# One decoder block on one core: every engine's calls in another sequence, and the table of logarithms read only when another was read since

## What is computed

```python
x = x + attention(layernorm(x))        # 16 heads of 32, one shared K and V, windows of 128 in steps of 64
x = x + wkv(w, u, layernorm(x), ctx)   # a recurrence over the tokens, per channel
x = x + ffn(layernorm(x))              # 512 -> 2048 -> 512
# attention, per window:
Q, K = Q * cos + rotate_half(Q) * sin, K * cos + rotate_half(K) * sin
K, V = quant_dequant_8bit(compress(K)), quant_dequant_8bit(compress(V))
p = sigmoid(Qw @ Kw.T * scale);  wout = p / (p.sum(-1) + 1e-8) @ Vw      # neighbouring windows are blended
# ffn: activations are rounded to 8 bits per row, weights to -1, 0, 1 by the mean of their magnitudes
h = silu(linear(x, w_gate)) * linear(x, w_up);  out = linear(rms_norm(h), w_down)
```

## Time and profile before

| what | value |
|---|---|
| runs | 1063.14, 1063.1 and 1060.24 us, median 1063.1 |
| profiled execution, its span | 1062.2 us |
| PE busy | 867.7 us (82%) |
| DVE busy | 854.9 us (80%) |
| ACT busy | 660.2 us (62%) |
| POOL busy | 454.9 us (43%) |

### The profile page before, as it was taken

The page is one execution under the profiler, slowest core; times in us unless marked ns, Lnnn a source line. Parts: engine busy times, 40 slices in busy tenths (PEclk is TensorE's granted clock), DMA queues, the critical chain, the costliest instruction groups (busy, mean ns, idle before and its releaser), DMA issues.

```text
span 1062.2 us, 22082 instructions
## 1 busy us (share of the span) xinstructions
PE 867.7 (82%) x8388; PEld 522.0 (49%) x8388; DVE 854.9 (80%) x1630; ACT 660.2 (62%) x1162; POOL 454.9 (43%) x494
## 2 busy tenths in 40 slices
PE   6984646769888889888888888888898988986665
PEld 3453434445555555555545555555555555553222
DVE  4766495998979897988979898979897879797944
ACT  0237654564949595858576767667676757584633
POOL 1111113155453645363636364646464535445522
PEclk9996667979999999999999999999999999998978
DMA  9977251210606151515142323232323223032032
GB/s 339 412 240 270 82 196 41 68 41 11 147 21 137 31 138 29 137 31 112 56 92 71 82 81 87 81 87 81 87 81 86 82 56 111 29 103 49 21 60 69
DMA packets 119386, 107.17 MB, mean 101 GB/s; under 512 B 91792, under 2 KB 94720, under 8 KB 118128
## 3 DMA queue, kind: packets, MB, share of 16 engines
q1 hardware_dynamic: 116320, 100.64, 32.6%
q0 software_dynamic: 624, 2.59, 0.8%
q10 hardware_dynamic: 2336, 2.52, 0.7%
HBM read 65.62 MB, written 10.75 MB: 72 GB/s over the span
## 4 chain that ended last, share of the span: by engine, by line
PE 43%; DVE 17%; ACT 15%; issue 11%; DMA 6%; POOL 2%; SPq 1%; DVEq 0%; ACTq 0%; POOLq 0%
PE bank L513 11%; PE bank L602 10%; PE bank L612 7%; PE bank L543 5%; PE bank L532 5%; ACT arena L742 3%; DMA wide<-wide 3%; ACT junk L799 2%; ACT junk L804 2%; DVE amax L1143 2%; DVE wide L1034 2%; DVE wide L1060 1%; DVE fs L1186 1%; PE bank L583 1%; ACT L742 1%
## 5 line engine op out<-in xcount | busy, mean ns | idle before, releaser
L602 PE MATMUL bank<-w_up_gate,qT 128*128 128x512 bf16 x1024 | 241.1, 387 | 28.3 <-DMA qT<-q_tok 22.0
L1378 POOL TENSOR_TENSOR work<-junk,lnw 128x512 f32<-128x512 f32 x128 | 180.7, 1431 | 183.5 <-DVE junk L1177 161.4
L602 PEld LDWEIGHTS bank<-w_up_gate,qT 128*128 128x128 bf16 x1024 | 98.7, 99 | 144.0 <-DMA qT<-q_tok 23.3
L513 PE MATMUL bank<-wide,wq_sb 128*128 128x256 f32 x512 | 131.1, 421 | 28.1 <-DVE rows L1078 28.1
L612 PE MATMUL bank<-w_down,work 128*128 128x512 bf16 x512 | 121.5, 383 | 22.5 <-ACT junk L799 13.3
L513 PEld LDWEIGHTS bank<-wide,wq_sb 128*128 128x128 f32 x512 | 107.8, 213 | 57.2 <-issue 39.7
L1177 DVE TENSOR_TENSOR junk<-bank,junk 128x512 f32<-128x512 f32 x128 | 86.2, 683 | 59.3 <-PE bank L602 55.5
L799 ACT ACTIVATE junk<-bank,deq 128x512 f32<-128x512 f32 x128 | 85.6, 686 | 72.2 <-PE bank L602 71.6
L742 ACT ACTIVATE arena<-bank 128x384 f32<-128x384 f32 x256 | 104.8, 496 | 33.7 <-PE bank L532 33.5
L532 PE MATMUL bank<-wide,k_win 32*128 32x128 f32 x1536 | 69.1, 315 | 61.3 <-ACT arena L742 38.2
L564 PE MATMUL bank<-wo_sb,wide 128*128 128x512 f32 x256 | 117.0, 611 | 2.5 <-DVE wide L1071 2.5
(11 more groups left out here) (154 smaller groups left out, 1478.0 us busy)
## 6 DMA issues: line engine op xcount, KB each, us to landing
sums<-in_xT SPq DMA_DIRECT2D x8, 1024.0 KB, 10.9
wide<-in_xT SPq DMA_DIRECT2D x16, 512.0 KB, 4.3
wide<-wide SPq DMA_DIRECT2D x64, 128.0 KB, 2.1
out<-rows SPq DMA_DIRECT2D x32, 256.0 KB, 2.3
ctx_T<-in_ctxT SPq DMA_DIRECT2D x15, 512.0 KB, 5.0
rows<-in_x SPq DMA_DIRECT2D x15, 512.0 KB, 3.2
kv_b<-k_raw SPq DMA_DIRECT2D x64, 96.0 KB, 2.4
work<-in_wgT SPq DMA_DIRECT2D x4, 1024.0 KB, 7.5
```

Source lines behind the costliest of these rows:

```text
L513: last = te.matmul(in_bank(k, 2)[:, n % 2, :], wq_sb[:, c, n * P:(n + 1) * P], xT[:, c, :], start=c == 0, stop=c == NC - 1)
L602: last = te.matmul(bank[4 + k % 4][:, :], qT[:, c, t * P:(t + 1) * P], w_up_gate[:, m, c, cols], start=c == 0, stop=c == NC - 1)
L1378: ge.tensor_tensor(hid_w[:, t, cols], hid[:, n % 2, :], lnw[:, cols], op=ALU.mult).then_inc(z_set.sem, 1)
```

## The change

Every engine gets its calls in another sequence; none is added or removed, but for table loads. `log_tables()` is now called by each function that needs the table (`logs`, `inverses`, `wkv_logs`, `wkv_inverses`, `exps`), and does nothing if that table was the last one read. The call stands ahead of the function's waits, as before.

```diff
+        held = [None]
+
         def probs(b, c):
+            held[0] = None
...
         def log_tables():
-            se.add_instruction(mybir.InstLoadActFuncSet(name=nc.get_next_instruction_name(),
-                                                        engine=mybir.EngineType.Activation, act_func_set_id=LN_EXP))
+            if held[0] != LN_EXP:
+                se.add_instruction(mybir.InstLoadActFuncSet(name=nc.get_next_instruction_name(),
+                                                            engine=mybir.EngineType.Activation, act_func_set_id=LN_EXP))
+            held[0] = LN_EXP
 
         def logs(b, c):
+            log_tables()
...
         def silu(f, t, n):
+            held[0] = None
```

On DVE, the tail of a round and the start of the next:

```diff
+            if i == 2:
+                round_weights(DOWN, 0)
             if do_f:
+                wkv_norm(f)
+            if do_g:
+                peak(g, 1)
+            if i == 2:
+                round_weights(DOWN, 1)
+            if do_f:
+                wkv_quantise(f)
...
+            if do_w:
+                residual(w)
...
+            if i == 2:
+                round_weights(DOWN, 2)
+            if do_w:
+                att_norm(w)
+            if do_f:
                 hidden(f, 0, 0)
+            if do_g:
+                hidden_round(g, 1)
...
+            if do_f:
+                hidden(f, 0, 1)
             if do_b:
                 rope(b, 0)
                 rope(b, 1)
...
+            if do_w:
+                scan(w, 0)
             if do_b:
                 rotate(b, 0)
-            if do_w:
-                scan(w, 0)
...
                 rotate(b, 1)
```

On POOL, the sum of the third weight:

```diff
             if do_f:
                 hidden_rstd(f, 0)
+            if i == 1:
+                weight_total(DOWN)
...
                 weigh_hidden(w, 0, 0)
-            if i == 0:
-                weight_total(DOWN)
-            if do_w:
                 weigh_hidden(w, 0, 1)
```

More of the change, by code:

```diff
@@ L621, in tensor_program @@
             do_b, do_w, do_f, do_g = [0 <= n < B for n in (b, w, f, g)]
+            if do_g:
+                gate_up(g, 1, 1)
+            if do_w:
+                nums(w, 2)
+            if do_g:
+                gate_up(g, 1, 2)
+            if do_w:
+                nums(w, 3)
+            if do_g:
+                gate_up(g, 1, 3)
+            if do_f:
+                wkv_back(f, 0)
+                wkv_back(f, 1)
+            if do_w:
+                attention_out(w, 0)
+                attention_out(w, 1)
             if do_b:
@@ L626, in tensor_program @@
                 gate_up(f, 0, 0)
+                gate_up(f, 0, 1)
             if do_w:
@@ L851, in scalar_program @@
             if do_b:
+                probs(b, 1)
                 probs(b, 2)
@@ L883, in scalar_program @@
                 silu(f, 1, 0)
[L884 to L893 removed]
+            if i == 1:
+                sum_weights(DOWN, 3)
+            if i == -2:
+                sum_weights(GATE, 2)
     def vector_program(ve):
```

287 lines of the change are left out of this document (128 added, 159 removed).

## The result

The changed kernel takes 1097.52 us, the median of four runs (1096.16 to 1098.32), beside 1061.97 for the kernel before. The ratio is 1.0328, with a 95% interval of 1.029 to 1.0367: slower by 35 us. The profiled execution has a span of 1094.9, 32.7 more than before.

The account below looks back on a forecast made before the run. No engine alone was taken to bound the kernel, but a loop through several. Rounds of 56.65 against 55.1, 13 times, gave +20, the fill +0.5, on 1062.2: 1083 us, range 1052 to 1098.

Parts of the forecast that it names:

- likeliest case: Whole kernel: longer rounds make it slower, 1083 us, own range 1074 to 1094, given 48%.
- 1.66 longer: Leg `hidden(1,0)` to `residual`, before 13.35: one `refine` (0.60) and one blend (1.20) move behind `hidden(1,0)`, less a 0.15 wait.
- Queries to `probs(0)`: First leg of a round: later `rope` and scans delay `scores(0)`, table load exposed; 0.78 us longer than 20.49.
- `probs(0)` to `probs(3)`: Second leg of a round: same calls of scores, down and probs alternate, so unchanged at 8.08 us.
- a slower clock behind that pause: Much slower rival: PE's pauses halve its clock in most rounds, over 1.2 us a round more, 1098 and above; 9%.
- `probs(3)` to `silu(1,0)` and to `hidden(1,0)`: Legs before `hidden(1,0)`: gaps between logarithms and inverses close, 0.61 us shorter; DVE then waits for silu alone, 0.32 shorter.
- The tables: First round: seven table loads go, 9.1 us less 0.6; queries of sequence 1 at 121.8 instead of 130.25, -8.5.
- the dearer price: First round: by the Trainium skill a table switch costs 2.66 us with its drain, so seven would be worth 18.6.
- The rest of the fill: Early rounds: `weight_total(DOWN)` +5, DVE's rounding +3.2, earlier third weight gains about 4; the fill comes to +0.5 us.
- The clock of queries: Middle rounds: queries at 8.83 us in every round because of longer pauses, adding 0.4 over the mean of before.

Follow-up runs that it names:

- x1: Changed kernel with DVE's first place as before (`rope` ahead of `hidden(0,1)`, first `rotate` ahead of the scans): 1086.63 us, ratio to before 1.0258.
- x6: Changed kernel with two of POOL's `weigh_hidden` multiplications cut to 64 of 512 columns, which alters the FFN's result: median 1086.82 us.
- y1: Kernel before with the rule for the table loads alone, every sequence as it was: 1052.35 us against 1059.89, ratio 0.9935.
- x5: Changed kernel with the round's tail as before on DVE (second place), ACT (`logs`, `inverses`) and PE (`nums`, `wkv_back`) together: 1081.37 us, ratio to before 1.0189.
- z1: Kernel before with DVE's first place alone as changed (`hidden(0,1)` ahead of `rope`, scans ahead of first `rotate`): 1074.98 us against 1062.81, ratio 1.0121.
- x2: Changed kernel with DVE's second place alone as before (both `refine` pieces and three blends ahead of `hidden(1,0)`): 1160.61 us, ratio to before 1.0952.
- z2: Kernel before with DVE's second place alone as changed (one `refine` and one blend behind `hidden(1,0)`): 1110.85 us against 1062.81, ratio 1.0469.
- z3: Kernel before with DVE's second place as changed and PE's `gate_up(1,3)` ahead of `wkv_back`: 1089.45 us against 1061.39, ratio 1.0273.
- x7: Changed kernel with the tail as before on DVE, ACT and PE, and DVE's first place as before too: 1073.3 us, ratio to before 1.0122.
- v1: Kernel before with the table rule, plus DVE rounding the third weight's pieces earlier, two of them ahead of `hidden(0,1)`: 1052.37 us.

## Why the prediction was right, and where it was off

The direction, the kind of case and the place were right: 1083 was forecast in a range of 1052 to 1098, and 1097.5 is at its upper edge, above the likeliest case's own 1074 to 1094. Two of the four runs (1098.29 and 1098.32) lie just above the range, so that the median is inside owes something to luck. A round was to grow by 1.55 (the terms as written add up to 1.6) and grew by 2.53. The step that failed is the term "1.66 longer" for `hidden(1,0)` to `residual`. It was mis-sized: 16.33 was measured, 2.98 over the calm round's 13.35 and 2.46 over the mean of before.

- **Queries to `probs(0)`.** Forecast q + 21.27 and +0.78; measured q + 21.0 to 21.14 with slow queries, +0.71 on the mean. Scores at q + 18.7 to 18.9 instead of 19.01. The pause of PE is 2.25, as said. The size was right, the reason only in part: I put `rope`'s late start down to `hidden(0,1)` ahead of it, and with that undone (x1) it still starts 0.85 late, behind `wkv_keys` on PE. Only 0.22 of the 0.65 at equal clock went with DVE's place.
- **`probs(0)` to `probs(3)`.** Forecast 8.08, measured 8.36. I had left a slower clock behind that pause out of the sum and in a rival. It came in a mild form, 0.42 in eight of twelve rounds. x1 removed the pause and the 0.28 with it.
- **`probs(3)` to `silu(1,0)` and to `hidden(1,0)`.** Forecast -0.61 and -0.32, measured -0.57 and -0.35.
- **`hidden(1,0)` to `residual`.** The moved work is there, but dearer than priced: the moved blend took 2.05 (696.35 to 698.40) instead of 1.20, the `refine` 0.95 instead of 0.60, and the last blend, which I didn't price, 1.34 instead of 0.98 (292.47 to 293.45). With POOL's `weigh_hidden` cut down the leg is 15.02 (x6), where 15.01 was forecast; the hundredth is luck, as the 0.35 of `refine` is still in it and as much went elsewhere. What I missed is the collision: I priced `blend_windows` with rows in which POOL did not touch it, and did not ask what POOL does at the blend's new time, though the round of 797.76 had the 1.42 in it. 1.3 x 13 = 17 us of the 35 come from it by the legs.
- **The tables.** Forecast -8.5, queries of sequence 1 at 121.8; measured 121.66. Alone in the kernel before, the rule is worth 7.5 us (y1). The 1.29 from a load to its activation held, and the first round got 8.3 shorter for seven loads (y1), far from the 18.6 that the dearer price would have given.
- **The rest of the fill.** Forecast +0.5 in all, measured +0.6, of which the parts are off by more and nearly cancel: sequence 2 at 188.1 forecast and 186.69 measured, the next round 0.8 longer forecast and 2.3 measured (65.00 for 62.66). `weight_total(DOWN)` did take POOL the reload:

```profile
171.60 0.40 POOL L1348 PARTITION_ALL_REDUCE abs_tot<-abs_sum  x1 [5.80 <-issue]
...
204.16 2.50 POOL L1384 TENSOR_TENSOR work<-junk,lnw 128x512 f32<-128x512 f32 x2 [6.59 <-issue]
```

5.80 us of issue, and DVE waited 5.35 for it. The third weight was ready earlier, and `weigh_hidden` started at 204.16 instead of 218.13.
- **The clock of queries.** I took queries at 8.83 in every round. They were mixed, as before: ten of twelve rounds of the slow kind (8.66 to 8.83 where the row holds all 32 matmuls) and two of 7.14. A pause of 2.93 does not settle it. That they could change between variants by far more, from 0 to 12 rounds at 7.14, was in no term of mine; in the changed kernel it cost nothing, in x5, x6 and z1 it moved the totals.

What "the same work, another order" hid: what the second place on DVE costs depends on what it meets. Undone alone it made the kernel 63 us slower, undone with its partners on ACT and PE 16 faster, and these 16 are queries at the higher clock, not shorter tail legs. That DVE's place at the head costs 8 to 11 in time is shown, and that POOL stretches the last leg by 1.3 a round. What POOL's own new order costs, and PE's head, is read from rows only, and the rest is open.

## What to carry to other kernels

An order that is spread over several engines is one object: test a part of it together with the calls it waits for and those that wait for it, or the part's own time can mislead (x2 beside x5, z2 beside z3). Compare the legs of a round and not the totals alone, at equal clock of TensorE: x5 was 16 us faster with tail legs of the same length. When an operation moves in time, price it with what the neighbours that share its memory ports do at the new time, not with its duration at the old. And a change that bundles a sure small gain (here the tables, 7.5 us) with a reordering is worth splitting, since the gain alone was the fastest kernel but for two variants that can't be told from it.

## What was not expected of the hardware

- A 128x192 addition of two on-chip tiles on VectorE took 1.42 us instead of 0.36 to 0.60 while GpSimd multiplied 128x512, and ended 0.2 us behind GpSimd's instruction; with GpSimd's cut to 64 columns it took 0.48; instructions beside it that read a bank kept their times.
- TensorE's clock behind a pause: after 2.25 us without work some scores took 1.37 instead of 0.95, but only in eight of twelve like rounds, and the queries behind equal pauses of 2.93 took 7.14 or 8.7 to 8.83. With pauses of 1.6 to 1.9 (x5, x7) they took 7.14 in 23 of 24 rounds. And the ten runs of v1 spread over 12 us, 1048.48 to 1060.38.
